# Softmax weights split before division: the row sums leave the probabilities, the head outputs take them, and the rotary arithmetic changes engine

## The chip, the core and the metric

The kernel runs on one core of a Trainium2 chip. The metric is the device time in microseconds (us) of one execution; lower is better. Engines are called by their names, and by the short names of the profile: TensorE (PE, its weight loads PEld), VectorE (DVE), ScalarE (ACT), GpSimd (POOL), SyncE (SP, which issues the DMAs). `L1234` is line 1234 of the kernel before.

## The reference

One pre-norm decoder layer for x of 4 batches, 512 tokens and 512 channels, in fp32: latent attention (16 heads), an int8-style quantised two-layer projection, and a top-2 mixture of 8 experts. The change concerns the attention alone:

```
q = rmsnorm(x @ w_qa, q_norm_w) @ w_qb        # 16 heads of 128 + 64 (rotary)
kv = rmsnorm(x @ w_kva ...) @ w_kvb           # 16 heads of 128 keys + 128 values
q_rope = q_rope * cos + rotate_half(q_rope) * sin
scores = einsum('blhd,bmhd->bhlm', q, k) / sqrt(192)
attn = softmax(where(causal, scores, -1e30), axis=-1)
out = einsum('bhlm,bmhd->blhd', attn, v)      # 4 x 16 heads
x = x + out.reshape(B, L, 16 * 128) @ w_o
```

## The kernel before, in words

Precision is kept by splitting each fp32 operand of a product into a high and a low fp16 half; a product is three matmuls (`TRI`: high by high, high by low, low by high). A half pair costs two passes: a copy that rounds (the high half), and a subtraction (the low half).

The kernel has three stages. A first one folds the head weights together. The second, the **walk**, does the attention: 32 pairs of heads (8 pairs in each of 4 batches), numbered i, with j = i mod 2; an "even pair" has j = 0. The third quantises, projects and runs the experts. The change lies in the walk.

A pair has two heads; a head has four groups g of 128 query rows, so a pair has groups 0 to 7, and group g has k + 1 blocks of 128 keys, k = g mod 4 (causal). For each group TensorE makes the scores (`scores`, L1933 to L1937, five matmuls) in one of three PSUM banks; VectorE masks and finds the row minimum of the negated scores (`row_max`, L1541, with an accumulator read behind it); ScalarE takes the exponential and its row sum (`exps`, L1241, with an accumulator read); VectorE makes the reciprocal (L1548), scales it by 4096 (L1550), multiplies the exponentials by it into the fp16 high halves (`probs_hi`, L1558) and the low halves (`probs_lo`, L1565); SyncE issues a DMA transpose of both (L1018). When a head's four transposes are in, TensorE multiplies by the latents (`values`, L1949), and the result is split by ScalarE (`out_hi`, L1248) and VectorE (`out_lo`, L1572). Eight split heads are then projected (`project`, L1964) and added to x (`add_y`, L1591).

Between the groups stand, in an order that is written out by hand for each engine as conditions on `(j, g)`:

- the next queries: `nope_mm` (L1912) on TensorE, split by ScalarE (`qn_hi_`, L1252) and VectorE (`qn_lo_`, L1577);
- the rotary part for the next pair: `rope_mm` (L1891) on TensorE; `rope_swap` (four copies of 32 partitions, L1261) on ScalarE; `rotate` (times cosine, L1585) on VectorE; `rope_sin` (L1087), `rope_sum` (L1093) and `rope_split` (L1098) on GpSimd; `rope_hi` (L1269 and four copies, L1273) on ScalarE;
- in pairs 0 to 23, the preparation of the next batch's tokens, one tile of 128 tokens for two pairs: `prep_mm` (L1858) and most of the rest in even pairs, the layer norm in odd ones. Pairs 24 to 31 have none.

TensorE starts a pair's first scores only when three things of this pair are there:

```
if k == 0:
    pe.wait_ge(qn_lo, 2 * i + h + 1)
if g == 0:
    pe.wait_ge(r_hi, i + 1)
    pe.wait_ge(r_split, i + 1)
```

and group G's scores wait for the exponential of group G - 3, which frees the bank. `values` waits for the transposes and, before the change, for `out_lo` of the head before, since there is one output bank.

Of the kernel before, what the change touches and what calls it, by code (L numbers as in the profile page):

```python
# [35 lines left out]
def decoder_layer(nc, x, fside, ctxw, w_qa, q_norm_w, w_qb, w_kva, kv_norm_w, w_kvb, w_o,  # L36
# [13 lines left out]

    x1_dram = nc.dram_tensor("x_after_attention", (B, L, D), fp32, kind="Internal").ap()

    with es:
# [23 lines left out]
        ARENA = 52400  # L77
# [3 lines left out]
        def take(cols, dt=fp32):  # L81
# [35 lines left out]
        XT = take(D)  # L117
# [5 lines left out]
        XN = take(D)  # L123
        XH = take(2 * D, fp16)
        XNT = take(2 * D, fp16)
        CF = take(QL + KVL)
        CH_AT = place[0]
# [6 lines left out]
        NB, SUM, RC, R4 = (small[:, 20 + 4 * k:24 + 4 * k] for k in range(4))  # L134
# [4 lines left out]
        square_out = take(QL + KVL, fp16)  # L139
# [39 lines left out]
            sem(n) for n in ("s_mm", "s_max", "s_exp", "s_rc", "s_hi", "s_lo"))  # L179
        pt_in = [sem(f"pt_in{k}") for k in range(TB)]  # L180
        s_r4 = sem("s_r4")
# [10 lines left out]
        S_BANKS, T_BANK, O_BANK, Y_BANK, Q_BANK, R_BANK, P_BANK = (0, 1, 2), 2, 3, 4, 5, 6, 7  # L192
# [778 lines left out]
        def _(sp):  # L971
# [40 lines left out]
            def turn_probs(i, g):  # L1012
# [5 lines left out]
                sp.dma_start_transpose(pt_blocks(g >> 2, k), ph(k)).then_inc(pt_in[k], 16)  # L1018

# [18 lines left out]
            for i in range(NPAIR):  # L1038
                for g in range(8):
                    if i % 2 == 1 and g == 6 and i // 2 + 5 < NT:  # L1040
                        turn_rows(i // 2 + 5)
                    if i % 2 == 0 and g == 3 and i // 2 + TB < NT:
                        turn_keys(i // 2 + TB)
                    if i % 2 == 0 and g == 4 and i // 2 + TB < NT:
                        turn_latents(i // 2 + TB)
                    turn_probs(i, g)
# [7 lines left out]
                    if i == NPAIR - 1 and g == 7:  # L1054
                        first_loads(sp)
# [4 lines left out]
        def _(pool):  # L1060
# [23 lines left out]
            def rope_sin(i):  # L1084

                pool.wait_ge(r_swap, i + 1)
                pool.tensor_tensor(RSW, RSW, SINT, ALU.mult).then_inc(r_sin, 1)  # L1087

            def rope_sum(i):

                pool.wait_ge(r_rot, i + 1)
                pool.wait_ge(r_sin, i + 1)
                pool.tensor_tensor(RT1, RT1, RSW, ALU.add).then_inc(r_sum, 1)  # L1093

            def rope_split(i, par):

                pool.wait_ge(r_own, i + 1)
                pool.tensor_tensor(QR[:, (par * 3 + 2) * L:(par * 3 + 3) * L], RT1, RHI, ALU.subtract).then_inc(r_split, 1)  # L1098

            def pair(i, j, first=False, last=False, prep=None, ahead=None):  # L1100
                for g in range(8):
                    if (j, g) == (0, 2):
                        if prep is not None:
                            prep_norm(prep[0])
                    if (j, g) == (0, 3):
                        if not last:
                            rope_sin(i + 1)
                    if (j, g) == (0, 5):
                        if not last:
                            rope_sum(i + 1)  # L1110
                    if (j, g) == (0, 6):
                        if not last:
                            rope_split(i + 1, 1 - j)
                    if (j, g) == (1, 3):
                        if not last:
                            rope_sin(i + 1)
                    if (j, g) == (1, 4):
                        if not last:
                            rope_sum(i + 1)
                    if (j, g) == (1, 5):  # L1120
                        if ahead is not None:
                            prep_rstd(ahead)
                        if not last:
                            rope_split(i + 1, 1 - j)
# [29 lines left out]
            pool.wait_ge(tab_made, 2)  # L1154
# [959 lines left out]
```

## Time and profile before

| what | value |
|---|---|
| median of 3 runs | 1166.24 us (1164.35 to 1167.4) |
| the profiled execution's own time | 1167.31 us |
| its span in the trace | 1165.5 us |
| PE busy | 957.6 us (82%) |
| DVE busy | 963.2 us (83%) |
| ACT busy | 643.6 us (55%) |
| POOL busy | 249.7 us (21%) |
| granted TensorE clock, mean | 0.93 |
| walk | from 162.6 us to about 850 us of the span |

Busy shares are means over the span. In the walk the two busiest engines are nearly equal, so the shares alone don't tell which one sets the pace; the starts of the pairs on TensorE and the waits in front of it do.

### The profile page before, as it was taken

What the parts mean: (1) busy time and instruction counts of PE and PEld (TensorE: products, weight loads), DVE (VectorE), ACT (ScalarE), POOL (GpSimd) and SP (SyncE); (2) the same over time, 40 slices, a digit from 0 to 9 for tenths busy, and PEclk for the clock granted to TensorE, in tenths of its full rate; (3) what the DMA queues carried; (4) which work ended last, traced back from release to release, by engine and by line L of the source; (5) the groups of instructions that cost most, each with busy time, mean ns of one, the idle gap of its engine ahead of it and who ended that gap; (6) DMA issues with size and microseconds to landing.
All of it is one profiled execution on the core that took longest, in us unless ns stands there. A gap on an engine that the chain in (4) does not pass through costs nothing.

```text
span 1165.5 us, 17748 instructions
## 1 busy us (share of the span) xinstructions
PE 957.6 (82%) x5622; PEld 546.8 (47%) x5640; DVE 963.2 (83%) x2902; ACT 643.6 (55%) x1437; POOL 249.7 (21%) x268
## 2 busy tenths in 40 slices
PE   0446567889999999999999999999978655559997
PEld 0324333554554555555555555555535444435553
DVE  5767748999888988998998988988968898857885
ACT  1446546666555656656656656666513675753442
POOL 1036522122112112212212212112100113221211
PEclk9769789999999999999999999999989888769999
DMA  9300004534433446443436433335364530002434
GB/s 346 145 1 1 10 8 85 93 76 80 94 67 78 81 78 154 84 74 78 88 77 151 77 70 68 68 63 136 71 212 109 146 103 6 1 0 37 80 85 91
DMA packets 247661, 98.19 MB, mean 84 GB/s; under 512 B 221832, under 2 KB 233096, under 8 KB 247056
## 3 DMA queue, kind: packets, MB, share of 16 engines
q1 hardware_dynamic: 247568, 97.06, 36.6%
q8 instruction: 46, 0.75, 0.3%
q14 instruction: 47, 0.39, 0.1%
HBM read 36.06 MB, written 7.34 MB: 37 GB/s over the span
## 4 chain that ended last, share of the span: by engine, by line
DVE 48%; PE 34%; ACT 7%; issue 6%; DMA 3%; POOL 2%; SPq 0%; DVEq 0%; ACTq 0%; POOLq 0%
PE bank L1964 8%; PE bank L1912 5%; DVE bank L1541 4%; DVE arena L1558 4%; PE bank L1858 4%; PE bank L1949 4%; DVE arena L1565 4%; DVE arena L797 3%; PE bank L1891 3%; DVE arena L715 2%; DVE arena L717 2%; DMA arena<-arena 2%; DVE arena L681 2%; DVE arena L1572 2%; DVE arena L1525 2%
## 5 line engine op out<-in xcount | busy, mean ns | idle before, releaser
L1241 ACT ACTIVATE arena<-bank,arena 128x128 f32<-128x128 f32 (+3 forms) x256 | 134.3, 525 | 108.2 <-DVE arena L1541 106.7
L1964 PE MATMUL bank<-arena 128*128 128x512 f16 x768 | 180.3, 383 | 1.9 <-DVE arena L1591 1.9
L1565 DVE SCALAR_TENSOR_TENSOR arena<-arena 128x128 f16<-128x128 f32 (+3 forms) x256 | 144.3, 564 | 9.1
L1541 DVE CUSTOM_DVE_ANT_0 bank<-bank,maskb,scal 128x128 f32<-128x128 f32 (+3 forms) x256 | 141.4, 552 | 12.1 <-PE bank L1937 11.6
L1949 PE MATMUL bank<-arena 128*128 128x512 f16 (+3 forms) x768 | 119.7, 308 | 33.6 <-DVE arena L1572 24.6
L1912 PE MATMUL bank<-arena 128*128 128x512 f16 x576 | 137.2, 384 | 0.0
L1949 PEld LDWEIGHTS bank<-arena 128*128 128x128 f16 x768 | 72.8, 100 | 92.9 <-issue 46.4
L1558 DVE TENSOR_SCALAR arena<-arena 128x128 f16<-128x128 f32 (+3 forms) x256 | 109.0, 426 | 7.3 <-DVE arena L1550 0.3
L1964 PEld LDWEIGHTS bank<-arena 128*128 128x128 f16 x768 | 74.0, 99 | 82.9 <-issue 6.0
L1087 POOL TENSOR_TENSOR arena<-arena 128x512 f32<-128x512 f32 x32 | 45.3, 1415 | 308.7 <-ACT arena L1261 308.5
L1261 ACT ACTIVATE arena<-bank 32x512 f32<-32x512 f32 x128 | 75.2, 588 | 30.9 <-PE bank L1891 29.6
L1252 ACT ACTIVATE arena<-bank 128x512 f16<-128x512 f32 x64 | 38.2, 597 | 92.8 <-PE bank L1912 92.4
L1933 PE MATMUL bank<-arena 128*128 128x128 f16 (+3 forms) x256 | 77.2, 301 | 9.7 <-DVE arena L1452 5.0
L1912 PEld LDWEIGHTS bank<-arena 128*128 128x128 f16 x576 | 57.1, 99 | 56.5 <-issue 3.5
L1273 ACT ACTIVATE arena<-arena 64x512 f16<-64x512 f32 x128 | 79.9, 624 | 1.1
L1934 PE MATMUL bank<-arena 128*128 128x128 f16 (+3 forms) x256 | 77.1, 301 | 0.0
L1935 PE MATMUL bank<-arena 128*128 128x128 f16 (+3 forms) x256 | 76.9, 301 | 0.0
L1936 PE MATMUL bank<-arena 128*128 128x128 f16 (+3 forms) x256 | 76.9, 300 | 0.0
L1937 PE MATMUL bank<-arena 128*128 128x128 f16 (+3 forms) x256 | 76.9, 300 | 0.0
L1858 PE MATMUL bank<-arena 128*128 128x384 f16 (+1 forms) x384 | 54.9, 304 | 20.2 <-DVE arena L1408 15.2
L841 PE MATMUL bank<-identf,arena 128*128 128x128 f32 x192 | 37.8, 356 | 40.9 <-DVE arena L727 36.1
L1891 PE MATMUL bank<-arena 128*128 128x512 f16 x288 | 67.4, 379 | 0.0
(200 smaller groups left out, 1892.8 us busy)
## 6 DMA issues: line engine op xcount, KB each, us to landing
arena<-arena SPq DMA_TRANSPOSE x308, 2.7
arena<-in_L_attn_w_qb SPq DMA_DIRECT2D x1, 4608.0 KB, 21.0
arena<-in_x SPq DMA_DIRECT2D x4, 1024.0 KB, 6.0
arena<-in_L_attn_w_o SPq DMA_DIRECT2D x1, 4096.0 KB, 31.4
arena<-in_fside_BxS2xS SPq DMA_DIRECT2D x4, 1024.0 KB, 8.2
arena<-in_L_ffn_w SPq DMA_DIRECT2D x8, 512.0 KB, 7.9
out<-arena SPq DMA_DIRECT2D x16, 256.0 KB, 2.4
arena<-in_x SPq DMA_DIRECT2D x12, 256.0 KB, 2.9
```

Of the source, the lines that this page charges most:

```text
L1241: act.activation(pf(k), banks[S_BANKS[G % 3]][:, 0:n].rearrange("p (t c) -> p t c", c=P), ACT.Exp, bias=NB[:, k:k + 1], scale=-1.0, accum_ ...
L1273: last = act.activation(QR[a:a + DR, o:o + L], RT1[h * DR:(h + 1) * DR, :], ACT.Copy)
L1541: dve.tensor_tensor_reduce(s, s, maskb[:, L - n:L], nsc_exp, 3e38, ALU.add, ALU.min, NB[:, (g & 3):(g & 3) + 1]).then_inc(s_max, 1)
L1558: dve.tensor_scalar(ph_part(k, 0), pf(k), R4[:, k:k + 1], None, ALU.mult).then_inc(s_hi, 1)
L1565: dve.scalar_tensor_tensor(out=ph_part(k, 1), in0=pf(k), scalar=R4[:, k:k + 1], in1=ph_part(k, 0), op0=ALU.mult, op1=ALU.subtract).then_in ...
L1858: last = pe.matmul(banks[bank][:, 0:wid], XNT[:, (a * DC + c) * P:(a * DC + c + 1) * P], WA[:, w:w + wid], start=(k == 0), stop=(k == 3 * ...
L1891: last = pe.matmul(banks[R_BANK][:, :], wr(b, c, i & 7), ct(bp, a, c, 0, L), start=(k == 0), stop=(k == 3 * QC - 1))
L1912: last = pe.matmul(banks[Q_BANK][:, :], wq(a, c, (i & 7) * 2 + h), ct(bp, b, c, 0, L), start=(k == 0), stop=(k == 3 * QC - 1))
L1933: pe.matmul(bank[:, 0:n], qn(h, 0, q, P), ct(bp, 0, QC, 0, n), start=True, stop=False)
L1934: pe.matmul(bank[:, 0:n], qn(h, 0, q, P), ct(bp, 1, QC, 0, n), start=False, stop=False)
L1949: last = pe.matmul(banks[O_BANK][:, kt * P:L], cn(bp, a, kt), pt(h, b, kt, kt * P, L - kt * P), start=(kt == 0 and n == 0), stop=(kt == TB ...
L1964: last = pe.matmul(banks[Y_BANK][:, :], ot(gp, a, k, (q & 3) * P, P), wo(b, gp * GH + k), start=(k == 0 and n == 0), stop=(k == GH - 1 and ...
```

## The change

The exponentials are no longer multiplied by the reciprocal of their row sum before they are split and turned. Both halves are made of the exponential times the constant 4096: the high half on ScalarE (`probs_hi` moves there, right behind `exps`), the low one on VectorE as before. One reciprocal for each head (128x4, `row_scale`) takes the place of eight small instructions. Since a row sum belongs to a query, and a query lies along the free axis of the head's output, the reciprocals are written to DRAM (`store_sums`, 128 pieces of 16 B) and read back by all partitions (`spread_sums`, 256 KB to `RB`), and VectorE multiplies the output by them in its PSUM bank (`out_norm`) ahead of `out_hi` and `out_lo`. Outputs now alternate between two banks, 3 and 7; the preparation's first product of later batches uses bank 3. The three rotary instructions of GpSimd move to VectorE. `XT` shares its place with `XN`, `square_out` with `CF`. The pieces below are, in this order, of SyncE, ScalarE, VectorE (the new `row_scale`, `out_norm`, `rotate` and `rope_split`) and TensorE (`values`, and `prep_mm`, which moves one group later in even pairs).

```
+            def store_sums(Hd):
+                sp.wait_ge(s_rc, Hd + 1)
+                sp.dma_start(rc_dram[Hd].rearrange("(q t) -> q t", t=TB),
+                             RC[:, (Hd & 1) * TB:(Hd & 1) * TB + TB]).then_inc(rc_out[Hd & 1], 16)
+            def spread_sums(Hd):
+                sp.wait_ge(rc_out[Hd & 1], 16 * (Hd >> 1) + 16)
...
+                sp.dma_start(RB[:, (Hd & 1) * L:(Hd & 1) * L + L],
+                             rc_dram[Hd].partition_broadcast(P)).then_inc(rc_in[Hd & 1], 16)
...
+                    if g in (3, 7):
+                        store_sums(2 * i + (g >> 2))
+                    if g == 5:
+                        spread_sums(2 * i)
+                    if g == 1 and i > 0:
+                        spread_sums(2 * i - 1)
                     turn_probs(i, g)
...
+            def probs_hi(i, g):
...
+                act.activation(ph_part(k, 0), pf(k), ACT.Copy, scale=PSCALE).then_inc(s_hi, 1)
             def out_hi(Hd):
-                act.wait_ge(pv_mm, Hd + 1)
+                act.wait_ge(o_nrm, Hd + 1)
...
-                dve.reciprocal(RC[:, k:k + 1], SUM[:, k:k + 1]).then_inc(s_rc, 1)
-                dve.tensor_scalar(R4[:, k:k + 1], RC[:, k:k + 1], PSCALE, None, ALU.mult).then_inc(s_r4, 1)
-                dve.tensor_scalar(ph_part(k, 0), pf(k), R4[:, k:k + 1], None,
-                                  ALU.mult).then_inc(s_hi, 1)
+            def row_scale(Hd):
+                dve.wait_ge(s_exp, 4 * Hd + 4)
...
+                dve.reciprocal(RC[:, h * TB:h * TB + TB], SUM[:, h * TB:h * TB + TB]).then_inc(s_rc, 1)
...
+            def out_norm(Hd):
+                dve.wait_ge(pv_mm, Hd + 1)
+                dve.wait_ge(rc_in[h], 16 * (Hd >> 1) + 16)
+                o = banks[O_BANKS[h]].rearrange("p (t q) -> p t q", t=TB)
+                dve.tensor_tensor(o, o, rb(h), ALU.mult).then_inc(o_nrm, 1)
...
                 dve.tensor_tensor(RT1, banks[R_BANK][:, :], COST, ALU.mult).then_inc(r_rot, 1)
+                dve.tensor_tensor(RSW, RSW, SINT, ALU.mult).then_inc(r_sin, 1)
+                dve.wait_ge(r_rot, i + 1)
+                dve.wait_ge(r_sin, i + 1)
+                dve.tensor_tensor(RT1, RT1, RSW, ALU.add).then_inc(r_sum, 1)
+            def rope_split(i, par):
+                dve.wait_ge(r_own, i + 1)
+                dve.tensor_tensor(QR[:, (par * 3 + 2) * L:(par * 3 + 3) * L], RT1, RHI, ALU.subtract).then_inc(r_split, 1)
...
-                if not (i == 0 and h == 0):
-                    pe.wait_ge(o_lo, Hd)
+                if Hd >= 2:
+                    pe.wait_ge(o_lo, Hd - 1)
...
-                    if (j, g) == (0, 2):
+                    if (j, g) == (0, 3):
                         if prep is not None:
                             if started(i - 5):
                                 pe.wait_ge(y_added, i - 4)
+                            if not first:
+                                pe.wait_ge(o_lo, 2 * i - 1)
                             prep_mm(prep[0])
```

The order of the work moves with it. **ScalarE, second half of an even pair with preparation**, from `rope_swap` to group 6. Before:

```order
L1261 ACTIVATE arena<-bank 32x512 x4
L1225 ACTIVATE arena<-bank,arena 128x384
L1226 ACTIVATE arena<-bank,arena 128x128
L1241 ACTIVATE arena<-bank,arena 128x128
L1248 ACTIVATE arena<-bank 128x512
L1252 ACTIVATE arena<-bank 128x512
L1241 ACTIVATE arena<-bank,arena 128x256
L1269 ACTIVATE arena<-arena 128x512
L1273 ACTIVATE arena<-arena 64x512 x4
L1232 ACTIVATE arena<-arena 128x2x128
L1241 ACTIVATE arena<-bank,arena 128x3x128
```

After (L1263 is `rope_swap`, L1235 `exps`, L1245 `probs_hi`, L1219 and L1220 `prep_scale`, L1254 `qn_hi_`, L1271 and L1275 `rope_hi`, L1250 `out_hi`):

```order
L1263 ACTIVATE arena<-bank 32x512 x4
L1235 ACTIVATE arena<-bank,arena 128x128
L1245 ACTIVATE arena<-arena 128x128
L1219 ACTIVATE arena<-bank,arena 128x384
L1220 ACTIVATE arena<-bank,arena 128x128
L1254 ACTIVATE arena<-bank 128x512
L1235 ACTIVATE arena<-bank,arena 128x256
L1245 ACTIVATE arena<-arena 128x2x128
L1271 ACTIVATE arena<-arena 128x512
L1275 ACTIVATE arena<-arena 64x512 x4
L1250 ACTIVATE arena<-bank 128x512
L1235 ACTIVATE arena<-bank,arena 128x3x128
```

Each exponential now has its copy behind it, and `out_hi` of the previous pair's second head stands behind `rope_hi` instead of ahead of it.

**VectorE, the same stretch.** Before, from `rotate` (L1585) to `qn_lo_` (L1577), the last of the pair's duties that the next pair's first scores wait for:

```order
L1585 TENSOR_TENSOR arena<-bank,arena 128x512
L1523 CAST arena<-arena 128x512
L1525 TENSOR_TENSOR arena<-arena 128x512
L1541 ISA bank,arena<-bank,maskb,scal 128x256
L1541 ISA arena 128x1
L1548 RECIPROCAL arena<-arena 128x1
L1550 TENSOR_SCALAR arena<-arena 128x1
L1572 TENSOR_TENSOR arena<-bank,arena 128x512
L1558 TENSOR_SCALAR arena<-arena 128x128
...
L1565 SCALAR_TENSOR_TENSOR arena<-arena 128x2x128
L1577 TENSOR_TENSOR arena<-bank,arena 128x512
```

After, the end of that stretch, from the row minimum of group 6 (L1543) on, with `probs_lo` L1558, `out_lo` L1573, `rope_split` L1597 and `qn_lo_` L1578:

```order
L1543 ISA bank,arena<-bank,maskb,scal 128x384
L1543 ISA arena 128x1
L1558 SCALAR_TENSOR_TENSOR arena<-arena 128x2x128
L1573 TENSOR_TENSOR arena<-bank,arena 128x512
L1597 TENSOR_TENSOR arena<-arena 128x512
L1578 TENSOR_TENSOR arena<-bank,arena 128x512
```

`out_lo`, which stood ahead of group 4's halves, is now the instruction in front of `rope_split` and `qn_lo_`. In the same way the preparation's key arithmetic (`prep_srq`, `prep_rope_sum`) moves from ahead of `rotate` to behind it, in front of group 5's row minimum.

## Rows read from the trace of the kernel before

**Rows 1.** Stretch: us, busy of PE, PEld, DVE, ACT, POOL; granted clock, DMA share, GB/s.
```profile
500.00:600.00 100.00, 96.12 (x572) 52.08 (x571) 89.45 (x286) 60.04 (x148) 21.17 (x19) 1.00 0.42 79
```
**Rows 2.** Timeline, first score matmul of pairs 0, 8, 16, 17, 24, 25, 26.
```profile
162.61 0.27 PE L1933 MATMUL bank<-arena 128*128 128x128 f16 x1 [5.05 <-DVE arena L1452]
...
334.64 0.22 PE L1933 MATMUL bank<-arena 128*128 128x128 f16 x1
...
515.89 0.22 PE L1933 MATMUL bank<-arena 128*128 128x128 f16 x1
...
540.16 0.22 PE L1933 MATMUL bank<-arena 128*128 128x128 f16 x1
...
693.42 0.22 PE L1933 MATMUL bank<-arena 128*128 128x128 f16 x1
...
712.97 0.22 PE L1933 MATMUL bank<-arena 128*128 128x128 f16 x1
...
733.32 0.22 PE L1933 MATMUL bank<-arena 128*128 128x128 f16 x1
```
**Rows 3.** What TensorE waited for, 163 to 850 us (total, times, longest).
```profile
PE bank L1949 <- DVE arena L1572: 24.6, 13, 2.8
```
**Rows 4.** Timeline of pair 16: rope_mm, swap, exp, rope_hi, values, qn_lo.
```profile
526.20 2.11 PE L1891 MATMUL bank<-arena 128*128 128x512 f16 x9
...
528.14 1.79 PE L1949 MATMUL bank<-arena 128*128 128x512 f16 x12
...
528.35 2.39 ACT L1261 ACTIVATE arena<-bank 32x512 f32<-32x512 f32 x4 [0.59 <-PE bank L1891]
...
535.02 0.47 ACT L1241 ACTIVATE arena<-bank,arena 128x256 f32<-128x256 f32 x1 [1.96 <-DVE arena L1541]
...
535.94 1.79 PE L1949 MATMUL bank<-arena 128*128 128x512 f16 x12 [1.62 <-DVE arena L1572]
...
536.00 2.54 ACT L1273 ACTIVATE arena<-arena 64x512 f16<-64x512 f32 x4
...
538.01 0.68 DVE L1577 TENSOR_TENSOR arena<-bank,arena 128x512 f16<-128x512 f32 x1
```
**Rows 5.** VectorE groups by shape (busy, mean ns of one).
```profile
L1548 DVE RECIPROCAL arena<-arena 128x1 f32<-128x1 f32 x256 | 40.7, 159 | 12.4 <-ACT arena L1241 12.0
L1558 DVE TENSOR_SCALAR arena<-arena 128x512 f16<-128x512 f32 x64 | 31.5, 492 | 2.3
L1558 DVE TENSOR_SCALAR arena<-arena 128x128 f16<-128x128 f32 x64 | 22.2, 346 | 1.7
L1585 DVE TENSOR_TENSOR arena<-bank,arena 128x512 f32<-128x512 f32 x32 | 21.9, 684 | 0.5
```
**Rows 6.** The low half of the latents on VectorE (min/median/max ns).
```profile
L1525 DVE TENSOR_TENSOR arena<-arena x16: 691/1636/1643, 45.9 to 666.7; 128x512 f16<-128x512 f32 x16
```
**Rows 7.** ScalarE copies from SBUF by shape (columns as in rows 5).
```profile
L1206 ACT ACTIVATE arena<-arena 128x512 f16<-128x512 f32 x16 | 9.9, 621 | 18.4 <-DVE arena L1472 18.4
...
L1232 ACT ACTIVATE arena<-arena 128x256 f16<-128x256 f16 x16 | 6.7, 416 | 9.3 <-DVE arena L1525 9.0
```
**Rows 8.** Stretches behind waits of 2.83 us and 2.33 us: granted clock (columns as in rows 1).
```profile
202.40:205.90 3.50, 3.45 (x18) 2.24 (x19) 3.38 (x12) 3.29 (x8) 0.31 (x1) 0.56 0.14 29
...
224.10:227.50 3.40, 2.24 (x17) 1.31 (x17) 3.25 (x11) 3.34 (x7) 1.21 (x1) 1.00 0.48 94
...
355.40:358.90 3.50, 3.50 (x16) 1.84 (x17) 3.33 (x11) 3.44 (x8) 1.21 (x1) 0.65 0.51 99
```
**Rows 9.** DMA issues: KB each, us to landing.
```profile
arena<-arena SPq DMA_TRANSPOSE x308, 2.7
...
arena<-in_x SPq DMA_DIRECT2D x12, 256.0 KB, 2.9
```
**Rows 10.** Timeline, `prep_srq` and `prep_rope_sum` of pair 16, first and last of seven.
```profile
528.25 0.22 DVE L1486 TENSOR_SCALAR arena<-arena,scal 128x2 f32<-128x2 f32 x1
...
529.36 0.22 DVE L1513 TENSOR_TENSOR arena<-arena 128x64 f16<-128x64 f32 x1
```

More of the change, by code:

```diff
@@ L116, in decoder_layer @@
         arena16 = arena[:, :].bitcast(fp16)
-        XT = take(D)
+        RB = take(2 * L)
         QN = take(2 * 2 * L, fp16)
@@ L133, in decoder_layer @@
         small = take(40)
-        NB, SUM, RC, R4 = (small[:, 20 + 4 * k:24 + 4 * k] for k in range(4))
+        NB, SUM, RC = small[:, 20:24], small[:, 24:32], small[:, 32:40]
         rstd = small[:, 10:11]
@@ L1287, in pair @@
                             rope_swap(i + 1)
+                    if (j, g) == (0, 4):
                         if prep is not None:
                             prep_scale(prep[0])
-                    if (j, g) == (0, 4):
-                        if not first:
-                            out_hi(2 * i - 1)
                         if not last:
@@ L1297, in pair @@
                             rope_hi(i + 1, 1 - j)
+                        if not first:
+                            out_hi(2 * i - 1)
+                    if (j, g) == (0, 6):
                         if prep is not None:
                             prep_cn(*prep)
-                    if (j, g) == (0, 7):
-                        out_hi(2 * i)
                     if (j, g) == (1, 0):
                         qn_hi_(2 * i + 1, 1)
+                        out_hi(2 * i - 2)
                     if (j, g) == (1, 2):
@@ L1309, in pair @@
                             qn_hi_(2 * i + 2, 0)
-                    if (j, g) == (1, 4):
-                        if not first:
-                            out_hi(2 * i - 1)
                     if (j, g) == (1, 5):
@@ L1379, in _ @@
             walk(pair)
+            out_hi(2 * NPAIR - 2)
             out_hi(2 * NPAIR - 1)
@@ L1599, in pair @@
                         if not first:
-                            row_scale(G - 1, 7)
-                            probs_hi(i - 1, 7)
+                            row_scale(2 * i - 1)
                             probs_lo(G - 1, 7)
+                            out_norm(2 * i - 2)
+                    if (j, g) == (0, 1):
+                        probs_lo(G + 0, 0)
+                        if not first:
                             out_lo(2 * i - 2)
-                    if (j, g) == (0, 1):
-                        row_scale(G, 0)
-                        probs_hi(i, 0)
-                        probs_lo(G, 0)
                         if started(i - 5):
@@ L1683, in pair @@
                             prep_xn(ahead)
-                        if not first:
-                            out_lo(2 * i - 1)
                     if (j, g) == (1, 6):
-                        row_scale(G + 5, 5)
                         if not last:
+                            rope_split(i + 1, 1 - j)
                             qn_lo_(2 * i + 2, 0)
-                        probs_hi(i, 5)
                         probs_lo(G + 5, 5)
+                        out_norm(2 * i - 1)
                     if (j, g) == (1, 7):
-                        row_scale(G + 6, 6)
                         if ahead is not None:
                             prep_lo(ahead)
-                        probs_hi(i, 6)
                         probs_lo(G + 6, 6)
+                        out_lo(2 * i - 1)
             def largest(dst, src):
@@ L1776, in _ @@
                     rotate(0)
+                if h == 15:
+                    rope_split(0, 0)
             walk(pair)
-            row_scale(8 * NPAIR - 1, 7)
-            probs_hi(NPAIR - 1, 7)
+            row_scale(2 * NPAIR - 1)
             probs_lo(8 * NPAIR - 1, 7)
+            out_norm(2 * NPAIR - 2)
             out_lo(2 * NPAIR - 2)
+            out_norm(2 * NPAIR - 1)
             out_lo(2 * NPAIR - 1)
@@ L1852, in prep_mm @@
                     pe.wait_ge(xn_in, 16 * (n - TB) + 16)
-                for lo, wid, bank, done in ((0, QL, P_BANK, qa_mm), (QL, KVL + DR, Y_BANK, kv_mm)):
+                for lo, wid, bank, done in ((0, QL, qa_bank(n), qa_mm), (QL, KVL + DR, banks[Y_BANK], kv_mm)):
                     k = 0
@@ L1980, in pair @@
                                 pe.wait_ge(y_added, i - 4)
+                            if not first:
+                                pe.wait_ge(o_lo, 2 * i - 1)
                             prep_mm(prep[0])
```

158 lines of the change are left out of this document (61 added, 97 removed).

## The prediction

> **What bounds the kernel now.** I read the stretches first, then the starts of the pairs on TensorE, then TensorE's waits, then the timeline of one pair. In the steady walk TensorE is 96% busy at the full clock, VectorE 89%, ScalarE 60% and GpSimd 21% [rows 1]: two engines are near their limit, and the reader should see that a relief of VectorE is worth only what TensorE loses to it. The starts of the pairs give that [rows 2]. Pairs 0 to 7 take 334.64 - 162.61 = 172.0 us. From pair 8 to 24 there are 358.8 us; an odd pair takes 733.32 - 712.97 = 20.35 us (the eight odd ones 162.8), so the eight even ones with preparation share 196.0, 24.5 each, and pair 16 takes 540.16 - 515.89 = 24.27. An even pair without preparation takes 712.97 - 693.42 = 19.55. TensorE's largest wait is `values` for `out_lo` of the head before: 24.6 us in 13 waits [rows 3], one of them 1.62 us in pair 16 [rows 4]. That is the stall that the second output bank takes away. Odd pairs have no such wait. So at most some 2.2 us of an even pair are to be had, and the early pairs, which have no projection yet, may gain more.
>
> **VectorE's load.** Per pair go 8 reciprocals and 8 scalings (159 ns each taken for both), 2.5 us, and 8 high halves, from 346 ns at 128 wide to 492 at 512 [rows 5]; with (346 + 492) / 2 as the mean, 3.4 us. Two wider reciprocals (0.3), two `out_norm` (2 x 0.68, as L1585, which also reads PSUM and SBUF) and three rotary instructions (3 x 0.69, the least of L1525, SBUF alone) come: 3.7 us [rows 5, 6]. Net 2.2 us less of some 19. Each is cover work as long as VectorE is not the one that is waited for. The strided read of `RB` is in no row; between 0.68 and twice that (the 1.64 us that L1525 takes at its median [rows 6] would be the far end), I take 0.68 as nothing in L1585's form says otherwise.
>
> **ScalarE's load.** Eight copies from SBUF come. A copy of 512 takes 621 ns, one of 256 takes 416 [rows 7]; on that line 384 takes 0.52 and 128 takes 0.31 or a little less. Two heads: 3.7 us per pair, on 12.9 (60% of 21.4): 16.6 of about 21. It fits, but the copies stand in line between an exponential and the rotary copies. The Trainium skill ("ScalarE: Activation LUTs", Rules for kernel authors) advises the opposite move, multiplications to VectorE, and budgets 0.3 us plus 0.83 ns per element on ScalarE. By that budget the eight cost 4.5 us and the chain below is 0.1 us longer, some 1.6 us over the walk; the copy rows are shorter and decide.
>
> **GpSimd and the queue.** GpSimd loses its three rotary instructions. While it ran them, L1525 took 1.64 us instead of 0.69 [rows 6], so the two were in each other's way; that gives VectorE back about a microsecond in a preparation pair. The Trainium skill ("SBUF — State Buffer", the shared port pair) calls this an exclusive lock between GpSimd and a VectorE instruction with two SBUF inputs; this trace agrees. SyncE gets four DMAs per pair. Both legs of the round trip are in no row: nearest are a 256 KB load, 2.9 us to landing, and a transpose, 2.7 [rows 9]; two such legs are 6 us, and twice that is the far bound. The reciprocal is made in group 4 and used in the next pair's group 0, some ten microseconds later, so I charge nothing; if the cover fails, `out_norm` holds VectorE for the rest.
>
> **The chain that I expect to bind.** This decides the sign. TensorE may start pair i + 1 only with `r_hi`, `r_split` and `qn_lo`. In pair 16 TensorE leaves `rope_mm` at 528.14, `qn_lo_` runs from 538.01 to 538.69, and TensorE starts pair 17 at 540.16 [rows 2, 4]: after `rope_mm` TensorE needs 12.0 us, 1.8 of them idle (the wait for `out_lo` and its start), so 10.2 of work, and the chain, 10.55, ends 1.5 us early. After the change the chain of an even pair is, each instruction behind the one before:
> - 0.2 until ScalarE sees the product, `rope_swap` 2.39, as now [rows 4];
> - `rotate`, product, sine product and sum on VectorE, the sum behind a wait: 0.60 + 0.60 + 0.75, 1.95 [rows 5, 6];
> - `prep_srq` and `prep_rope_sum`, which now stand behind `rotate`: 528.25 to 529.50, 1.25 [rows 10];
> - the row minimum of group 5, 0.57; its exponential, 0.60; its new copy, 0.33 until the next one starts [rows 4, 7];
> - `rope_hi`, 3.06: 0.52 from the exponential's end, then 2.54 [rows 4];
> - `out_hi` 0.60, and on VectorE `out_lo` 0.65, `rope_split` 0.60, `qn_lo_` 0.68 [rows 4, 5].
>
> Together 12.9 us against 10.2 of TensorE's work: TensorE stalls 2.7 us at the end of the pair. The stall for `out_lo` goes, this one comes. **Even pairs with preparation:** from the start to the end of `rope_mm` TensorE takes 12.25 us in pair 16 [rows 2, 4]; `prep_mm` now waits also for `out_lo` of the previous pair's first head, which waits for `out_hi`, which stands behind `qn_hi_`; I add 0.45. 12.7 + 12.9 = 25.6, against 24.5: 8 x 1.1 = 8.8 us slower. **Even pairs without preparation:** the chain lacks the 1.25, 11.65 us. Up to `rope_mm`'s end the work is 8.8 us (19.55 less 10.2, less the idle 0.5). But ScalarE reaches the swap late: exponential and copy of groups 2 and 3 have to follow VectorE, which waited in group 1 for `out_hi`; I estimate 1.7 us. 8.8 + 1.7 + 11.65 = 22.2 against 19.55: 4 x 2.6 = 10.6 us. **Odd pairs:** the same chain is about 19.7 us from the start, `out_hi` is behind it and `prep_srq` absent: hidden by TensorE's 20.35, nothing. **Pairs 0 to 7:** odd ones gain about 2 us each while nothing is projected, even ones lose up to 3 like the rest; 172 becomes 176, 4 us slower, by the same steps. **Ends:** three instructions more on VectorE before the first pair, two of them ahead of its last head products, which TensorE waits 5.05 us for [rows 2], 1.3 us; an `out_norm` more behind the last `values`, 0.7. Sum: 8.8 + 10.6 + 4 + 2 = 25 us.
>
> **The clock.** Behind a wait of 2.83 us the granted clock was 0.56 for 3.5 us, that is the 1.2 GHz level for most of it; behind one of 2.33 us it was once 0.65 and once full [rows 8]. Half speed for 3.4 us costs 1.7 us of TensorE's work. The stalls above are 2.7 to 3.4 us, once in each of the 16 even pairs. From none to all, 0 to 27 us; since these rows show both outcomes near this length I take half, 8 x 1.7 = 14.
>
> Total: +39 us on the profiled execution's 1167.3 (span 1165.5), 1206; the median of the runs is 1.1 lower, so **1205 us**.
>
> **Rivals.**
> 1. *TensorE's own work binds, faster.* If the chain overlaps better than I add up (under 12.0 us from `rope_mm`'s end to `qn_lo_`, which is the point where it decides), even pairs fall to 22.1 (24.27 less 2.2), early ones with VectorE's 2.2 to 3 us: 8 x 2.4 + 8 x 2 = 35 us, 1132; half of it, 1148, is likelier. For it: VectorE is lighter, 24.6 us of waits go, and GpSimd's interference ends. Against: the move of `out_lo` and `prep_rope_sum` into the chain. Chance 0.17.
> 2. *No change to speak of:* the new stall just replaces the old one, 1166. An even pair would be 24.3 with a chain of 11.7. Chance 0.07.
> 3. *Every stall drops the clock:* 1166 + 25 + 27 = 1218. Chance 0.2; my own case is its milder form, 0.5.
> 4. *The round trip through DRAM binds:* if both legs take double, 12 us against 10, 2 us for each head where VectorE has no slack, 1230 or more. The DMA share is 0.42 [rows 1], so it is no full queue. Chance 0.06.
>
> **Numbers.** Faster by over 0.3% (3.5 us, about what a measurement can tell here from no change): 0.17; within it 0.07; slower 0.76. The range, 1160 to 1225, takes in the chain without any loss of clock (1191), all of rival 3, no change, and leaves out most of rivals 1 and 4. My own case alone would be 1190 to 1215.
>
> **What would show it.** In the profile after: VectorE down by some 70 us, ScalarE up by 118, GpSimd down by 120; no wait of `values` for `out_lo`; in its place TensorE waits in front of the score matmuls of odd pairs for `qn_lo_`, 2 to 3 us each; even pairs of 25 to 26 us and late ones of 22, odd ones of 20.4 or, with the clock fallen, 22; half-clock stretches behind the stalls. If the score matmuls of odd pairs wait for nothing and even pairs take 22 us, the chain was wrong and rival 1 right. If `out_norm` is seen waiting for a DMA, it is rival 4.

## The result, and the profile after

| | before | after |
|---|---|---|
| median | 1165.49 us (4 runs) | 1230.78 us (4 runs, 1229.62 to 1232.31) |
| ratio | | 1.0559, 95% interval 1.0539 to 1.0579 |
| span of the profiled execution | 1165.5 us | 1229.5 us |
| PE, DVE, ACT, POOL busy, us | 957.6, 963.2, 643.6, 249.7 | 974.5, 889.0, 759.9, 126.6 |

The change costs 65 us. The forecast was 39 us and a range that ended at 1225, so the direction was right and the size was not. The busy times moved as forecast: VectorE 74 us less (70 expected), ScalarE 116 more (118), GpSimd 123 less (120). The kernel has less to do on the engine that was its busiest, VectorE, and is 5.6% slower.

The steady walk after the change, in the columns of [rows 1]:

```profile
500.00:600.00 100.00, 91.00 (x518) 48.27 (x517) 72.68 (x191) 69.54 (x168) 2.51 (x4) 0.95 0.47 95
```

No engine is near its limit now: TensorE fell from 96 to 91, VectorE from 89 to 73. A stretch in which every engine has room and the time still grew is one in which they wait for each other. What TensorE waited for in the walk (total, times, longest), against [rows 3]:

```profile
PE bank L1926 <- DVE arena L1578: 29.3, 13, 5.3
PE bank L1957 <- DVE arena L1573: 27.8, 7, 4.1
PE bank L1851 <- DVE arena L1603: 9.7, 9, 1.1
PE bank L1926 <- ACT arena L1275: 7.6, 3, 2.9
```

L1926 is the first score matmul and L1578 `qn_lo_`: the stall that was forecast in place of the one for `out_lo`, of which nothing is left in front of `values` (L1942). L1957 is `project` and L1573 `out_lo`: seven waits of up to 4.1 us that the prediction does not have. L1851 is `prep_mm` and L1603 `add_y`; L1275 is the end of `rope_hi`.

The starts of pairs 14 to 17 on TensorE, the counterpart of [rows 2]:

```profile
495.63 0.22 PE L1926 MATMUL bank<-arena 128*128 128x128 f16 x1
...
521.77 0.23 PE L1926 MATMUL bank<-arena 128*128 128x128 f16 x1 [2.73 <-DVE arena L1578]
...
543.81 0.22 PE L1926 MATMUL bank<-arena 128*128 128x128 f16 x1
...
573.84 0.26 PE L1926 MATMUL bank<-arena 128*128 128x128 f16 x1
```

Pair 14 takes 26.14 us, pair 15 22.04, pair 16 30.03. There are two kinds of even pairs where there was one. Read over the whole walk (from pair 0 to pair 31: 670.1 us before, 734.7 after, 64.6 more, so the walk holds all of it):

| pairs | before | after | more | forecast without clock |
|---|---|---|---|---|
| 0 to 7 | 172.0 | 186.6 | 14.5 | 4 |
| 8, 12, 16, 20 | 99.4 | 118.4 | 19.0 | 4.4 |
| 10, 14, 18, 22 | 96.6 | 104.6 | 8.0 | 4.4 |
| 24, 28 | 39.2 | 50.2 | 11.1 | 5.3 |
| 26, 30 | 39.1 | 45.7 | 6.6 | 5.3 |
| odd, 9 to 29 | 223.9 | 229.3 | 5.4 | 0 |

The chain of pair 14, the counterpart of [rows 4]; L1263 is `rope_swap`, L1588 and L1592 `rotate`'s product and sum, L1515 the end of `prep_rope_sum`, L1275 `rope_hi`, L1250 `out_hi`:

```profile
508.65 1.79 PE L1942 MATMUL bank<-arena 128*128 128x512 f16 x12
508.85 2.39 ACT L1263 ACTIVATE arena<-bank 32x512 f32<-32x512 f32 x4 [0.52 <-PE bank L1884]
...
511.37 0.69 DVE L1588 TENSOR_TENSOR arena<-bank,arena 128x512 f32<-128x512 f32 x1 [2.32 <-ACT arena L1263]
...
512.76 0.69 DVE L1592 TENSOR_TENSOR arena<-arena 128x512 f32<-128x512 f32 x1
...
514.48 0.22 DVE L1515 TENSOR_TENSOR arena<-arena 128x64 f16<-128x64 f32 x1
...
516.64 2.53 ACT L1275 ACTIVATE arena<-arena 64x512 f16<-64x512 f32 x4
...
519.19 0.60 ACT L1250 ACTIVATE arena<-bank 128x512 f16<-128x512 f32 x1
...
519.82 0.69 DVE L1573 TENSOR_TENSOR arena<-bank,arena 128x512 f16<-128x512 f32 x1 [1.55 <-ACT arena L1250]
...
520.43 0.68 DVE L1597 TENSOR_TENSOR arena<-arena 128x512 f16<-128x512 f32 x1
...
521.03 0.69 DVE L1578 TENSOR_TENSOR arena<-bank,arena 128x512 f16<-128x512 f32 x1
```

From the end of `rope_mm` (508.65) to the next pair's scores (521.77) are 13.12 us; 12.9 were forecast, and the instructions are those that the prediction lists, in its order. VectorE idles 1.55 us ahead of `out_lo`, with `rope_split` and `qn_lo_` queued behind it although both could run: `rope_split` needs the first copy of `rope_hi`, done at 516.7, and `qn_lo_` the copy `qn_hi_`, done at 515.0.

The same point of pair 16, in the timeline:

```profile
568.00 0.69 DVE L1573 TENSOR_TENSOR arena<-bank,arena 128x512 f16<-128x512 f32 x1 [1.56 <-ACT arena L1250]
...
568.75 5.29 PE L1957 MATMUL bank<-arena 128*128 128x512 f16 x12 [4.12 <-DVE arena L1573]
```

And the changed kernel's stretches behind the stalls of pairs 14 and 16 (columns as in [rows 1]; the granted clock is the third figure from the right, 0.63 and 0.50):

```profile
521.80:525.30 3.50, 3.50 (x17) 1.87 (x18) 2.92 (x8) 2.07 (x6) 0.00 (x0) 0.63 0.59 84
...
568.75:573.80 5.05, 5.05 (x12) 1.78 (x13) 2.28 (x5) 2.18 (x5) 0.00 (x0) 0.50 0.46 97
```

`project(i - 4)` starts a group of eight heads in pairs 4, 8, ..., 28, and its line `pe.wait_ge(o_lo, 8 * (q >> 2) + 8)` asks for all eight, the last of which is the previous pair's second head, `out_lo(2i - 1)`. Before, that stood in group 5; now it is at the pair's end. TensorE sits idle for 4.12 us, and then does the twelve matmuls at the 1.2 GHz level, 5.29 us instead of 2.75. The same twelve before the change, in pair 16, with no wait:

```profile
537.57 2.75 PE L1964 MATMUL bank<-arena 128*128 128x512 f16 x12
```

Behind pair 14's stall of 2.73 us the clock was 0.63 over 3.5 us.

### The profile page after: what moved, and what is told of

Read it like the earlier page. It is cut to its first block, busy times and chain, and to the rows that moved or that the text cites. A ratio compares the mean times of both kernels' runs of the same rounds, so it can differ in the third digit from the quotient of the medians.

```text
span 1229.5 us, 17681 instructions
## 1 busy us (share of the span) xinstructions
PE 974.5 (79%) x5622; PEld 550.8 (45%) x5640; DVE 889.0 (72%) x2358; ACT 759.9 (62%) x1693; POOL 126.6 (10%) x172
## 4 chain that ended last, share of the span: by engine, by line
DVE 37%; PE 28%; ACT 17%; issue 11%; DMA 3%; POOL 2%; SPq 1%; DVEq 0%; ACTq 0%; POOLq 0%
PE bank L1957 8%; PE bank L1905 4%; ACT arena L1275 4%; PE bank L1851 4%; ACT arena L1263 3%; DVE arena L808 3%; PE bank L1884 3%; ACT arena L1250 3%; DVE bank L1543 2%; DVE arena L726 2%; ACT arena L1235 2%; DVE arena L728 2%; DVE arena L1573 2%; DVE arena L692 2%; DVE arena L1558 2%
## 5 line engine op out<-in xcount | busy, mean ns | idle before, releaser
L1957 PE MATMUL bank<-arena 128*128 128x512 f16 x768 | 194.5, 405 | 29.7 <-DVE arena L1573 27.8
L1235 ACT ACTIVATE arena<-bank,arena 128x128 f32<-128x128 f32 (+3 forms) x256 | 134.5, 525 | 123.8 <-DVE arena L1543 122.3
L1543 DVE CUSTOM_DVE_ANT_0 bank<-bank,maskb,scal 128x128 f32<-128x128 f32 (+3 forms) x256 | 141.5, 553 | 20.9 <-PE bank L1930 20.8
L1558 DVE SCALAR_TENSOR_TENSOR arena<-arena 128x128 f16<-128x128 f32 (+3 forms) x256 | 124.4, 486 | 26.2 <-ACT arena L1245 26.1
L1905 PE MATMUL bank<-arena 128*128 128x512 f16 x576 | 139.8, 389 | 0.0
L1957 PEld LDWEIGHTS bank<-arena 128*128 128x128 f16 x768 | 76.6, 103 | 120.0 <-DVE arena L1573 29.0
L1245 ACT ACTIVATE arena<-arena 128x128 f16<-128x128 f32 (+3 forms) x256 | 120.3, 470 | 8.1
L1942 PE MATMUL bank<-arena 128*128 128x512 f16 (+3 forms) x768 | 115.7, 301 | 9.9 <-DMA arena<-arena 8.6
L1926 PE MATMUL bank<-arena 128*128 128x128 f16 (+3 forms) x256 | 78.4, 306 | 43.8 <-DVE arena L1578 29.3
L1942 PEld LDWEIGHTS bank<-arena 128*128 128x128 f16 x768 | 72.5, 98 | 63.4 <-issue 9.8
L1573 DVE TENSOR_TENSOR arena<-bank,arena 128x512 f16<-128x512 f32 x64 | 44.2, 690 | 69.1 <-ACT arena L1250 68.4
L1905 PEld LDWEIGHTS bank<-arena 128*128 128x128 f16 x576 | 58.0, 101 | 58.9 <-issue 6.6
L1263 ACT ACTIVATE arena<-bank 32x512 f32<-32x512 f32 x128 | 75.3, 588 | 10.0 <-PE bank L1884 8.7
L1275 ACT ACTIVATE arena<-arena 64x512 f16<-64x512 f32 x128 | 79.8, 624 | 1.2
L1927 PE MATMUL bank<-arena 128*128 128x128 f16 (+3 forms) x256 | 78.2, 306 | 0.0
L1928 PE MATMUL bank<-arena 128*128 128x128 f16 (+3 forms) x256 | 78.1, 305 | 0.0
L1851 PE MATMUL bank<-arena 128*128 128x384 f16 (+1 forms) x384 | 55.3, 305 | 28.6 <-DVE arena L1410 15.8
L1929 PE MATMUL bank<-arena 128*128 128x128 f16 (+3 forms) x256 | 78.0, 305 | 0.0
L1930 PE MATMUL bank<-arena 128*128 128x128 f16 (+3 forms) x256 | 77.9, 304 | 0.0
L1568 DVE TENSOR_TENSOR bank<-bank,arena 128x512 f32<-128x512 f32 x64 | 69.0, 1078 | 4.9 <-PE bank L1942 4.0
L1254 ACT ACTIVATE arena<-bank 128x512 f16<-128x512 f32 x64 | 38.1, 596 | 54.1 <-PE bank L1905 54.1
L551 ACT ACTIVATE arena<-arena 128x512 f32<-128x512 f32 (+1 forms) x64 | 34.1, 603 | 58.1 <-DVE arena L730 57.9
```

What stands on the lines that cost most here:

```text
L1235: act.activation(pf(k), banks[S_BANKS[G % 3]][:, 0:n].rearrange("p (t c) -> p t c", c=P), ACT.Exp, bias=NB[:, k:k + 1], scale=-1.0, accum_ ...
L1245: act.activation(ph_part(k, 0), pf(k), ACT.Copy, scale=PSCALE).then_inc(s_hi, 1)
L1263: last = act.activation(RSW[a + o:a + o + 32, :], banks[R_BANK][a + 32 - o:a + 64 - o, :], ACT.Copy)
L1275: last = act.activation(QR[a:a + DR, o:o + L], RT1[h * DR:(h + 1) * DR, :], ACT.Copy)
L1543: dve.tensor_tensor_reduce(s, s, maskb[:, L - n:L], nsc_exp, 3e38, ALU.add, ALU.min, NB[:, (g & 3):(g & 3) + 1]).then_inc(s_max, 1)
L1558: dve.scalar_tensor_tensor(out=ph_part(k, 1), in0=pf(k), scalar=PSCALE, in1=ph_part(k, 0), op0=ALU.mult, op1=ALU.subtract).then_inc(s_lo, 1)
```

## The experiments

Ratios are to the kernel before, on the same chip, with 95% intervals. The edits of e1 to e4 are made to the changed kernel.

**e1, the projection's wait.**

```
-                    pe.wait_ge(o_lo, 8 * (q >> 2) + 8)
...
                 for k in heads:
+                    pe.wait_ge(o_lo, 8 * (q >> 2) + k + 1)
```

> The changed kernel, in which the projection of a head waits for out_lo of that head alone and not, at a group's first head, for all eight heads of the group. Theory (a missed wait): in pairs 4, 8, 12, ..., 28 the projection behind group 7 is held until out_lo of the previous pair's second head, which the change moved to the end of the even pair; those seven pairs fall from 28.4 to 30.0 us (25.9 and 24.3 for pairs 24 and 28) to the 26.1 (22.9) of their neighbours, 21 us less in all, some of which comes back as half-clock stretches in the odd pairs behind them (1.7 us each): 1210 to 1216 us. Rival (the seven pairs are long because the clock falls there, or because of their preparation): the wait moves to the scores of the next pair and the time stays at 1226 to 1231.

Measured: 1218.29 us, 1.0461 (1.0411 to 1.0511), 12.5 us less. Pairs 8, 12, 16 and 20 fall from 29.10 to 30.04 us to 26.13 to 26.16, the same as their neighbours, and pairs 24 and 28 to 22.84 and 22.85. The missed wait is shown: the seven pairs are 21 us shorter, and the rival (1226 to 1231 us) is out. Less came through than I expected, 1218.3 against 1210 to 1216: in 9 of the 11 odd pairs from 9 to 29 TensorE now loses about 1.3 to 1.7 us to the half clock (21.67 to 22.04 us instead of 20.35), since each of them starts behind a stall. Between 170 and 850 us of the span the granted clock is at half for 51.2 us here and in the changed kernel. Pair 16 of e1, where `project` no longer waits and the scores of pair 17 do:

```profile
560.94 2.75 PE L1957 MATMUL bank<-arena 128*128 128x512 f16 x12
566.42 0.29 PE L1926 MATMUL bank<-arena 128*128 128x128 f16 x1 [2.73 <-DVE arena L1578]
```

**e2, the order at the end of even pairs.**

```
                         probs_lo(G + 5, 5)
-                        if not first:
-                            out_lo(2 * i - 1)
                         if not last:
                             rope_split(i + 1, 1 - j)
                             qn_lo_(2 * i + 2, 0)
+                        if not first:
+                            out_lo(2 * i - 1)
```

> The changed kernel with one move on VectorE in group 6 of even pairs: rope_split and qn_lo go ahead of out_lo. Theory (the chain from the rotary product to qn_lo sets even pairs): the chain then ends with rope_hi, 2.6 us earlier, so the nine even pairs that don't wait for a whole group of heads go from 26.1 to about 23.6 (22.9 to 20.3), the seven others stay: 23 us and a few half-clock stretches less, 1200 to 1208 us. Rival (ScalarE's eight new copies and total load bind): the order of three VectorE instructions moves nothing, 1226 to 1231.

Measured: 1211.2 us, 1.04 (1.0351 to 1.0449), 19.6 less; a little short of the expected 23, and 3 us above the expected range. Pair 14 takes 23.89 (26.14 before the edit), pair 26 20.49 (22.86), pair 15 20.36 (22.04), and pair 16 still 29.94. The order of three VectorE instructions moved what ScalarE's load, the rival, could not explain. What is left of the stall ahead of pair 15:

```profile
513.47 0.23 PE L1926 MATMUL bank<-arena 128*128 128x128 f16 x1 [0.48 <-DVE arena L1578]
```

**e3, both.**

> Both edits together. Theory: they are two separate stalls of the same pairs, so the sum is at least the sum of both, about 62 us with all sixteen even pairs relieved, and the half clock in the walk goes as well, up to 7 us: 1158 to 1172 us. Rival (load of ScalarE, or the half clock, sets a floor): not below 1190.

Measured: 1174.7 us, 1.0073 (1.0046 to 1.0101), 56.1 less, above the upper end of my expectation by 2.7. Alone the edits gave 12.5 and 19.6, together 56.1: each alone left the other stall in the same or the neighbouring pair, and with it the half clock, which is down from 51 us to 14 (between 170 and 850 us of the span). The trace splits the 24 us that the sum of both lacks: the seven long pairs (4, 8, ..., 28) became 21 us shorter in e1 and 2 us longer in e2, and 37 us shorter with both edits, 18 us more than the sum; the rest is mostly the odd pairs, which e1 alone had made longer. So one wait and one place in the order, with no piece of arithmetic more or less, hold 56 of the 65 us.

**e4, the stride of `out_norm`.**

```
-            return RB[:, h * L:(h + 1) * L].rearrange("p (q t) -> p t q", t=TB)
+            return RB[:, h * L:(h + 1) * L].rearrange("p (t q) -> p t q", t=TB)
```

> The changed kernel whose out_norm reads the reciprocals side by side instead of 16 bytes apart (they are then applied to the wrong queries; the amount of work is the same). Theory: the stride is why out_norm takes 1.08 us and not 0.69; it is off the end-of-pair chain and stands only ahead of the preparation's wait for out_lo, so at most 0.4 us per even pair, 1224 to 1229 us. Rival (VectorE's load counts): 64 x 0.39 us, 25 us less, about 1206.

This kernel leaves out the right pairing of reciprocals and queries; its work is the same. Measured: 1224.48 us, 1.0514 (1.0454 to 1.0574), 6.3 less. The two kernels' `out_norm` (min/median/max ns), changed and e4:

```profile
L1568 DVE TENSOR_TENSOR bank<-bank,arena x64: 1046/1074/1149, 190.3 to 924.3; 128x512 f32<-128x512 f32 x64
```

```profile
L1568 DVE TENSOR_TENSOR bank<-bank,arena x64: 687/691/700, 190.4 to 917.5; 128x512 f32<-128x512 f32 x64
```

The stride is the 0.38 us; 64 x 0.38 would be 24.5 us, so at most a quarter was on the path. The even pairs with preparation that don't wait in `project` fell by 0.4 us each (pair 14 from 26.14 to 25.74), where `prep_mm` waits. Some 3.4 of the 6.3 us are not the stride itself: behind the same stalls of 2.7 us the clock fell ahead of pairs 15 and 19 in the changed kernel and did not in e4 (20.36 instead of 22.04 us each).

Next, three edits to the kernel of e3.

**e5, the key arithmetic behind group 4's low half.** `prep_rope_sum` moves from (0, 4) to (0, 5), behind `probs_lo(G + 4, 4)`.

> The kernel of e3 with prep_rope_sum (the key arithmetic, 1.1 us) moved on VectorE from ahead of group 5's row minimum to behind group 4's low half, and the keys' transpose one group later on SyncE. Theory (chain): the 1.1 us leave the chain, but since out_lo and qn_lo are already off its end only the remaining 0.7 us of stall in each of 12 even pairs with preparation can go: 23.9 to 23.2 us, 1164 to 1169 us. Rival (after e3 the load of VectorE sets the pair): unchanged, 1172 to 1176.

Measured: 1171.39 us, 1.0054 (1.0034 to 1.0075), 3.3 less in the medians, which is not clear of noise (e3's interval reaches down to 1.0046), and even pairs stay at 23.88. A miss. The step was no longer ahead of `rope_hi`, but it was still ahead of `qn_lo_` on VectorE, which runs without a gap from 578.65 to 584.6 in pair 18: with the chain through ScalarE shortened, VectorE's own line was the next limit.

**e6, the three rotary instructions back on GpSimd.** `rope_sin` and `rope_sum` in group 4, `rope_split` in group 6 of both kinds of pairs.

> The kernel of e3 with the three rotary instructions back on GpSimd. Theory (chain): 2.8 us on GpSimd run beside 1.9 us of other VectorE work, so the chain to rope_hi is shorter by about what e5 takes out, and the low half of the latents is slowed to 1.6 us again: 1163 to 1172 us. Rival (VectorE's load binds): 2 us less per pair show in the early pairs as well, below 1155. Rival (GpSimd's 3.9 us are in the chain): above 1185.

Measured: 1162.13 us, 0.9962 (0.9951 to 0.9973): 12.6 below e3, a little below the expected range, and a little below the kernel before. Even pairs with preparation 23.3, early ones 0.2 to 1.1 us shorter. I had expected the low half of the latents to be slowed again; it was not (693 ns on average), but `probs_lo` at 256 columns was, from 417 ns to 652.

**e7, the high halves back on VectorE**, unnormalised: `tensor_scalar` by 4096 in front of `probs_lo`, and no copies on ScalarE.

> The kernel of e3 with the high halves back on VectorE (unnormalised). Theory (chain): the copies of groups 3 to 5 leave ScalarE's line (1.2 us in an even pair), but VectorE gets 8 instructions of 0.3 to 0.5 us and reaches about 90% again, so pairs 0 to 7 and the row minima get later: 1172 to 1190 us. Rival (ScalarE's copies are what costs): 1155 to 1165.

Measured: 1179.42 us, 1.0118 (1.0085 to 1.0151), 4.7 above e3, with intervals that overlap a little (e3's ends at 1.0101); even pairs with preparation 24.5 instead of 23.9 in the trace, VectorE at 90% again. Moving the copies to ScalarE seems to be worth a little; that it was the cost, the rival (1155 to 1165), is ruled out.

**e8, `rope_hi` ahead of group 5's exponential**, an edit to e5 (in even pairs `qn_hi_` also goes ahead of `prep_scale`).

> The kernel of e5 with rope_hi ahead of group 5's exponential on ScalarE, in even and odd pairs. Theory (chain): rope_hi needs only the rotary sum; row minimum, exponential and copy of group 5 (1.5 us) leave the chain, the waits for L1275 (7.6 us in pairs 0 to 7) and the rest of the end-of-pair stalls go; even pairs with preparation 22.9 to 23.2 us: 1152 to 1163 us, for the first time at or below the kernel before. Rival: exponentials get late instead and scores wait for banks, no gain over e5.

Measured: 1176.54 us, 1.0088 (1.0055 to 1.0121). A miss: slower than e5 by 5 us. Odd pairs 1 and 3 gained 1.8 us each, but even ones went from 23.88 to 24.13 and from 20.49 to 21.64, all waiting for `qn_lo_` (29.4 us in 22 waits). I read it so, without a further run: the exponential of group 5 came later and with it VectorE's queue, in which `qn_lo_` stands last.

**e9, `qn_lo_` of the second head first**, an edit to e6: ahead of `out_lo` and `add_y` in group 1.

> The kernel of e6 with qn_lo of a pair's second head ahead of out_lo and add_y on VectorE (group 1 of both kinds of pairs). Theory (chain): the scores of the second head no longer wait for it (1.26 us in each late even pair of e3), late even pairs fall from 20.5 to 19.3, the rest gains 0 to 0.3 us per pair because the row minimum of group 2 comes 0.6 us sooner: 1153 to 1159 us. Rival: out_lo gets later by as much and prep_mm waits for it, no change, 1160 to 1164.

Measured: 1163.8 us, 0.9985 (0.9973 to 0.9996), not below e6 (1162.13). The late even pairs fell as expected, from 20.5 to 19.5, and most of the ones with preparation rose from 23.3 to 23.45 or more, since `prep_mm` waits longer for `out_lo` and `add_y` (12.2 us in 11 waits instead of 8.9). Theory and rival were each right in one kind of pair.

**e10, reciprocals scattered on the way out**, an edit to e9, so that e4's side-by-side read keeps the right order:

```
-                sp.dma_start(rc_dram[Hd].rearrange("(q t) -> q t", t=TB),
+                sp.dma_start(rc_dram[Hd].rearrange("(t q) -> q t", t=TB),
```

> The kernel of e9 with the reciprocals stored in DRAM in the order of the queries (512 pieces of 4 bytes), so that out_norm reads side by side and stays correct. Theory: 0.2 to 0.4 us less on VectorE for each head, seen at prep_mm only, and a longer store that is covered: 2 to 5 us below e9. Rival: the 4-byte pieces hold up SyncE's transposes, and values or the high halves wait for DMA: above e9.

Measured: 1530.73 us, 1.3131 (1.3103 to 1.316). The rival, and far beyond what I had in mind. Landing times of the store (L1033), in the changed kernel and in e10:

```profile
DMA to landing us min/median/max: 1.4/2.0/3.9
```

```profile
DMA to landing us min/median/max: 8.7/11.0/15.2
```

And of the probabilities' transposes (L1028) on the same queue, in the changed kernel and in e10:

```profile
DMA to landing us min/median/max: 2.3/3.0/5.8
```

```profile
DMA to landing us min/median/max: 2.4/5.1/8.3
```

`values` (L1956) waits for these transposes, 9.1 us in all in e9 and in e10:

```profile
PE bank L1956 <- DMA arena<-arena: 319.4, 56, 13.2
```

**e11, the key arithmetic really behind `qn_lo_`**, an edit to e9: `prep_rope_sum` in group 7, and the DMA transpose of the keys with it.

> The kernel of e9 with the key arithmetic of VectorE behind group 7's work instead of group 4's, so really behind qn_lo, which e5 did not do. Theory (e5 gained nothing since the 1.1 us stayed ahead of qn_lo on the same engine): even pairs with preparation lose their last 0.3 to 0.5 us of stall, 12 pairs, 3 to 6 us below e9. Rival (it only moves the backlog into the next pair): equal to e9.

Measured: 1155.28 us, 0.9907 (0.9887 to 0.9926), 8.5 below e9, more than the 3 to 6 expected, and faster than the kernel before by 10 us. Even pairs with preparation mostly 22.95 (24.27 before the change), pair 0 21.5, pairs 1 and 3 19.5 and 19.4; half-clock time between 170 and 850 us of the span 7 us.

**e12, e11 with the rotary instructions on VectorE**, as the change has them.

> The kernel of e11 with the three rotary instructions on VectorE, as the change has them. Theory (what is left in VectorE's line ahead of qn_lo counts): sine product and sum are 1.3 us that stand between the swap and group 5's row minimum, rope_split 0.6 us more; even pairs with preparation take 0.3 to 0.6 us longer than in e11 and the early ones up to 1 us: 1159 to 1168 us. Rival (GpSimd's slower instructions and its hold on VectorE cost as much as they save): equal to e11, 1152 to 1157.

Measured: 1180.29 us, 1.0131 (1.0103 to 1.0159): 25 us above e11, twice what I allowed. Even pairs with preparation 23.82, 0.9 more and not the 0.3 to 0.6 expected; and the odd pairs from 5 to 21 also rise, from 20.35 to 21.25 or more. The end of pair 17 in e12 shows where: the exponential of group 5 (L1235) waits for VectorE's row minimum (L1543), `rope_hi` comes behind it, and the scores of pair 18 start when it ends.

```profile
610.07 0.47 ACT L1235 ACTIVATE arena<-bank,arena 128x256 f32<-128x256 f32 x1 [3.05 <-DVE arena L1543]
...
611.51 2.53 ACT L1275 ACTIVATE arena<-arena 64x512 f16<-64x512 f32 x4
...
614.14 0.22 PE L1927 MATMUL bank<-arena 128*128 128x128 f16 x1 [0.74 <-issue]
```

My reading, which no run separates, is that the late key arithmetic is carried into the odd pair, where with the rotary work in VectorE's line there is no room to catch up. Stretch 500 to 600 us of e11 and of e12:

```profile
500.00:600.00 100.00, 97.47 (x578) 52.88 (x577) 80.66 (x206) 78.58 (x190) 20.12 (x19) 1.00 0.54 104
```

```profile
500.00:600.00 100.00, 95.26 (x565) 51.40 (x564) 79.17 (x214) 76.83 (x185) 2.51 (x4) 1.00 0.52 102
```

VectorE is 81% busy in one and 79% in the other, and the busier one is the faster. The share doesn't tell which is slower; what stands in front of what does.

## Why the prediction was right in its direction and wrong in its size

**Right: the chain that I expected to bind.** It was forecast at 12.9 us and measured 13.12; the stall behind it at 2.7 and measured 2.73; an even pair with preparation at 25.6 and measured 26.14, an even one without at 22.2 and measured 22.86. In the latter the chain was cut too short, 11.65 us against 12.59, while the part up to `rope_mm` was 0.2 us shorter than forecast. e2 and e3 show that it is this chain: with `out_lo` behind `qn_lo_` the pairs fall by 2.3 us.

**Wrong: the step "The stall for `out_lo` goes, this one comes".** It went in front of `values` and came back in front of `project`, 27.8 us in seven waits, a term that the prediction put at nothing without a reason. I followed `o_lo` to `values` and to `prep_mm` and not to its third user, `project`, whose wait stands in the code of the kernel before. It never cost anything there, so no row showed it. The seven pairs in which a group of eight heads begins exceed their neighbours by 21.1 us (2.8 in pair 4, 13.8 in pairs 8 to 20, 4.5 in pairs 24 and 28). Of these, some 10 us are longer waiting (27.8 us, where the neighbours' stalls of 2.73 and 2.20 us would come to 18), and 11.5 are the half clock in the twelve matmuls behind the waits, which took 30.8 us instead of 7 x 2.75. e1, which takes the wait away, gains 12.5 us, since the clock then falls in the odd pairs instead. 1205 and 21.1 would be 1226, but that counts part of the clock twice (14 us of it are in the 1205) and comes near the result partly by luck; by e1's 12.5 it would be 1218. What then is left, 13 us, lies mostly in pairs 0 to 7 (some 8 us) and in the other even pairs, which are about half a microsecond longer than forecast.

**Odd pairs and pairs 0 to 7, mis-sized.** I let the early odd pairs gain 2 us each while nothing is projected. Pairs 1 and 3 took 20.80 and 20.73 (21.05 and 20.03 before), and in e1, without the missed wait, 21.97 and 20.34; pair 5 took its old 20.35. Pairs 0 to 7 cost 14.5 us instead of 4. The starts put 3.9 of it in pair 2, 5.7 in pair 4 (2.8 of that the missed wait), 1.9 in pair 6 and 1.7, the clock, in pair 7. e3 takes 8.9 of the 14.5 away; what holds the other 5.6 I did not separate. The 2 us for both ends of the walk did not come: outside the walk the changed kernel is 0.6 us shorter.

**The clock, near in size and not in place.** 14 us were forecast for stalls at the end of all sixteen even pairs, 27 at most. In seven of them the wait in `project` came instead, and two are pairs 0 and 2. Behind the seven end-of-pair stalls of 2.73 and 2.20 us that were left, the clock fell five times; the four odd pairs of the walk that show it (7, 15, 19, 27 at 22.04) lose 1.7 us each, as forecast. Between 170 and 850 us of the span the granted clock is at half for 51.2 us, in the kernel before for 13.7: 37.5 us more at half speed, at most 19 us of work. The part outside these odd pairs lies inside six of the seven long pairs, as in pair 16, and in pairs 2 and 3.

**`out_norm`, mis-sized.** Taken at 0.68 us with 1.64 as the far end; measured 1.08. e4 puts its cost at 6 us at most, some 3 of it by way of the clock. I had said that nothing in L1585's form speaks for more; the 16-byte step did.

**ScalarE's copies.** Measured 0.31, 0.42, 0.52 and 0.63 us for 128 to 512 columns, on the line drawn from the rows. The Trainium skill's advice against such copies on ScalarE ("ScalarE: Activation LUTs", Rules for kernel authors) is not borne out in this kernel: e7, which follows it, is 4.7 us slower than e3, though the intervals overlap a little.

**GpSimd's interference.** L1525 fell from 1636 to 693 ns, as expected (L1527 after). That gain was worth less than GpSimd's work: e6 brings GpSimd back and gains 12.6 us. The Trainium skill describes an exclusive lock between the two engines ("SBUF — State Buffer", the shared port pair), and e11's trace agrees: the low half of the latents takes 1297 ns there on average and 692 in e12, and `probs_lo` at 128 columns 511 against 290. Even so, e11 against e12 shows that work beside VectorE's line is worth 25 us here, these slower instructions included.

**The rivals.** Rival 2, no change, did not come. Rival 4, the round trip: the two legs landed in 2.0 and 3.4 us, and `out_norm` waited for a DMA once, 0.8 us, so it is covered. Rival 1, a faster kernel, is what e11 gives, but only with another order and the rotary work on GpSimd. Rival 3 was nearest in number, 1218, and that is luck: it has every stall drop the clock and no wait in `project`.

## What to carry to other kernels

When a step is moved later on its engine, look up every waiter of its semaphore in the code, those too that never wait in the trace: a coarse wait that was free is the first to cost. In an order written by hand, put what the next stage waits for ahead of what waits itself; an in-order engine that idles in front of one instruction with ready ones behind it is the place to look. Two stalls of the same stage can hide each other: here the two edits gave 12.5 and 19.6 us apart and 56 together, so an edit that gives little alone is not yet shown to be small.

## What the hardware showed that I had not expected

- The same store of 2 KB in 512 pieces of 4 bytes instead of 128 of 16 bytes landed in 11.0 us instead of 2.0, delayed the transposes on the same queue from 3.0 to 5.1 us, and `values` waited 319 us for them; the kernel took 1531 us instead of 1164 (e10 against e9; e10 also has e4's read in `out_norm`, which was the faster one there).
- A VectorE product in PSUM whose second operand is read with a step of 16 bytes took 1074 ns for 512 columns, with adjacent elements 691 (e4).
- The same idle stretch of TensorE does not always cost the clock. Behind the stalls of 2.72 to 2.74 us ahead of an odd pair the granted clock fell to half, for 3.4 us, in ten of ten cases in e1, in three of five in the changed kernel and in one of five in e4; behind those of 2.06 to 2.20 us in six of eight. In e1 nine odd pairs from 9 to 29 became 1.3 to 1.7 us longer by it.
